# Which place of a step may take the next score product for a maximum, in the first unit of an attention stage

## The chip, the cores and the metric

The kernel runs on one core of one Trainium2 chip. The metric is the device time of one execution, in microseconds (us). It computes two transformer-like layers; the change touches one stage of the first, its attention. The engines in play are TensorE (PE; its weight loads are listed apart as PEld), VectorE (DVE), ScalarE (ACT), GpSimd (POOL) and the queues that issue DMA transfers, among them SyncE's (SP).

## The reference, cut to what matters

The first layer's attention works on x of 2 batches x 2048 tokens x 256, with 16 heads of 16 columns and 32 rotary columns that all heads share:

```
k = (c_kv @ W_k_up).reshape(Bb, Tt, NH, HD);  v = ...;  q = ...
scores = einsum('bqhd,bkhd->bhqk', q, k)
scores = scores + einsum('bqr,bkr->bqk', q_rope, k_rope)[:, None]
scores = scores / sqrt(HD + D_R)
scores = where(causal, -inf, scores)
w = softmax(scores, axis=-1)
attn = einsum('bhqk,bkhd->bqhd', w, v)
return attn @ W_o
```

The softmax is causal: a query sees the keys up to its own. A softmax may subtract any number of a row before the exponential, and this kernel subtracts a row's maximum of approximate scores.

## The kernel before, in words

**Units and steps.** `phase_attention` (from L632) goes over 8 units, each one batch and one group of four heads. The 2048 queries of a unit are four chunks of 512. A unit has 40 steps (`NS`); a step is one chunk `qc` of queries against one block `kb` of 128 keys. The chunks come in the order 2, 3, 1, 0 in all units but the second (unit 1), which has 3, 2, 1, 0 (`ORDER`). So in unit 0 steps 0 to 11 belong to chunk 2, steps 12 to 27 to chunk 3, steps 28 to 35 to chunk 1, and steps 36 to 39 to chunk 0. The last four steps of a chunk lie on the diagonal and have only 512, 384, 256 and 128 columns of queries.

**What TensorE does in a step.** `scores(s, 0)` and `scores(s, 1)` make the transposed scores of two heads each: two matmuls by L1055 and one by L1059 for each of the two heads. The two heads take the upper and the lower 64 rows of the array (in code r = 0 and r = 1), so matmuls of different halves run side by side. Then `weighted` (L1037) multiplies the exponentials of the step before with the values; it needs all 128 rows, so both halves must be through. ScalarE's exponential (L1097) reads the scores, and GpSimd masks the diagonal blocks (L898).

**Maxima ahead.** The number subtracted has to be in the operands before a chunk's first scores. So for each chunk TensorE also makes plain score products (L999), one matmul per pair and half, each into one of three PSUM banks used in turn (`RING` = 3). VectorE reduces each of them to a row maximum (L1175, or L1172 on the diagonal) and so sets its bank free. A unit has 80 pairs (i, block of queries, chunk of keys), so 160 of these products; I call one of them an item, and write 33b for the second half of pair 33. When a chunk's items are reduced comes its turn: VectorE folds them (L1182), TensorE transposes them (L1010), VectorE writes them as f16 (L1186), and the SP queue moves them by DMA into the operands (`shift`, L940 by the trace). The chunk's first scores wait for that DMA (L1055 behind `shift_ld`). All matmuls are in one stream in program order, so a waiting one holds all behind it.

**The planner.** Which item stands at which place of the stream is worked out when the kernel is built, by `schedule()` (from L691). It walks through all steps with a clock `now`, a time `rows[r]` at which each half of the array is through, and a time `reduced` at which VectorE is through with the items so far. `bank_free(slot)` is the time at which the bank of the item three before was reduced, plus 60; `begin_of(x)` is that for an item, and `reduced + 350` for a turn. A step has the places 0 to 7: place 0 ahead of it, places 1 to 6 behind its six pairs of score matmuls (3 and 6 are behind the last of `scores(s, 0)` and `scores(s, 1)`), place 7 behind `weighted`. At each place it issues items as long as they fit: an item behind a score matmul fits if its bank is free by the time its own half is through. At place 6, ahead of `weighted`, an item of the second half fits if its bank is free within 300 of that, and one of the first half if its bank is free within 100 and the bank after it already. If a chunk's turn isn't there when its first step comes, the planner issues all that is missing at place 0, adds 6500 (`FETCH`) for the DMA, and fills the wait with more items. Items of the next unit are allowed from step 6 on (`HEAD_STEP`), up to the end of its second chunk (`AHEAD`). `TODO` holds the result; TensorE (`ahead`, L1012) and VectorE (`ahead`, L1189) both follow it.

In this plan unit 0 opens with items 0a to 30b ahead of step 0, has from then on four items in nearly every whole step (one at place 5, three at place 7), and for step 12 (chunk 3's first) issues five items and the turn at place 0. It ends with 36b of unit 1. Unit 1 ends with 37a of unit 2, unit 2 with 41b of unit 3, and unit 3 with 42a of unit 4. In unit 2 the turn of chunk 3 stands at place 7 of step 10; in units 3 and on at step 7.

Of the kernel before, what the change touches and what calls it, by code (L numbers as in the profile page):

```python
# [631 lines left out]
def phase_attention(nc, g):  # L632
# [17 lines left out]
    def upto(v, m):  # L650
        return sum(2 * TPC * (qc + 1) for qc in ORDER[v][:m])
# [13 lines left out]
    def width(v, k):  # L665
        _, qb, j = PAIRS[v][k]
        return min(CH, (qb + 1) * P - j * CH)
# [10 lines left out]
    def chunk_maxima(v, m):  # L678
        return [("max", v, k, r) for k in range(upto(v, m), upto(v, m + 1)) for r in range(2)]
# [3 lines left out]
    def ticks(w):  # L683
        return w * 0.4167

    def reduce_time(v, k):
        if v == 0 and k in LIFTED:
            return 420
        return width(v, k) / 0.96 + (76 if diagonal(v, k) else 70)

    def schedule():  # L691

        stream = []
        for v in range(NU):
            for m in range(NCH):
                stream += chunk_maxima(v, m) + [("turn", v, m, 0)]
        todo, at = {}, 0
        now = reduced = 0.0
        rows, freed, turned_at = [0.0, 0.0], [], {}

        def may(u, s):
            if at == len(stream):
                return False
            kind, v, n, _ = stream[at]
            return v <= u or (v == u + 1 and s >= HEAD_STEP and n < (AHEAD if kind == "turn" else upto(v, AHEAD)))

        def bank_free(slot):
            return freed[slot - RING] + 60 if slot >= RING else 0.0

        def begin_of(x):  # L710
            return reduced + 350 if x[0] == "turn" else bank_free(len(freed))

        def issue(place):
            nonlocal at, now, reduced
            x = stream[at]
            kind, v, n, r = x
            todo.setdefault(place, []).append(x)
            at += 1
            if kind == "turn":
                now = max(now, *rows, begin_of(x)) + 64  # L720
                rows[:] = now, now
                reduced = max(reduced, now + 400) + 300
                turned_at[v, n] = reduced
                freed.extend([reduced] * (2 if n == NCH - 1 else 1))
            else:
                now = max(now, rows[r], begin_of(x))
                rows[r] = now + ticks(width(v, n)) + 5
                reduced = max(reduced, rows[r] + 217) + reduce_time(v, n)
                freed.append(reduced)

        for u in range(NU):
            for s in range(NS):
                qc, kb = STEPS[u][s]
                t = kb - TPC * qc
                w = CH - max(t, 0) * P
                if kb == 0:
                    m = ORDER[u].index(qc)
                    while (u, m) not in turned_at:
                        issue((u, s, 0))
                    ready = turned_at[u, m] + FETCH  # L740
                    while may(u, s) and max(now, *rows, begin_of(stream[at])) + 300 < ready:
                        issue((u, s, 0))
                    rows[:] = max(rows[0], ready), max(rows[1], ready)
                for i in range(1, 8):
                    if i == 7:
                        now = max(now, *rows) + 200 + ticks(4 * w)
                        rows[:] = now, now
                    else:
                        for r in sorted((0, 1), key=lambda r: rows[r]):
                            now = max(now, rows[r])  # L750
                            rows[r] = now + ticks(w)
                    while may(u, s):
                        x = stream[at]
                        if x[0] == "turn":
                            fits = begin_of(x) <= max(rows)
                        elif i != 6:
                            fits = begin_of(x) <= max(now, rows[x[3]])
                        elif x[3] == 1:
                            fits = begin_of(x) <= max(now, rows[1]) + SLACK + 200
                        else:  # L760
                            fits = begin_of(x) <= max(now, rows[0]) + SLACK and bank_free(len(freed) + 1) <= max(now, rows[0])
                        if not fits:
                            break
                        issue((u, s, i))
        return todo

    TODO = schedule()

    with ExitStack() as c:
# [2033 lines left out]
```

How the kernel before makes its waits and increments, by code:

```python
    def link(self, ins):  # L65
        ins.then_inc(self.sem, 1)
        self.n += 1
        self.eng.wait_ge(self.sem, self.base + self.n)
# [8 lines left out]
def ln_rows(dve, chain, x, tile0, hn, ln, b, it):  # L77
    for t in range(TPC):
        ins = dve.bn_stats(ln.st[:, t, :], x[:, tile0 + t, :])
    chain.link(ins)
    dve.memset(ln.gap[:, :], 0.0)
    for t in range(TPC):
        ins = dve.bn_aggr(ln.mv[:, t, :], ln.st[:, t, :])
    ins.then_inc(ln.var_ready[b], 1)
    dve.wait_ge(ln.root_ready[b], it + 1)
    chain.link(dve.reciprocal(ln.rs[:, :], ln.sd[:, :]))
    for t in range(TPC):
        ins = dve.tensor_scalar(hn[:, t, :], x[:, tile0 + t, :], ln.mv[:, t, 0:1], ln.rs[:, t:t + 1],
                                ALU.subtract, ALU.mult)
    return ins
# [2 lines left out]
def ln_root(act, ln, eps, b, it):  # L95
    act.wait_ge(ln.var_ready[b], it + 1)
    act.activation(ln.sd[:, :], ln.mv[:, :, 1], ACT.Sqrt, bias=eps[:, 0:1]).then_inc(ln.root_ready[b], 1)
# [60 lines left out]
def all_stored(eng, g, kinds, chunks):  # L159
    for kind in kinds:
        for x in range(2):
            eng.wait_ge(g.stored[kind][x], 16 * STORES[kind] * chunks)
# [66 lines left out]
        def own_stored(eng, kind, n):  # L230
            if n >= 2:
                eng.wait_ge(stored[kind][n % 2], 16 * STORES[kind] * (n // 2))
# [23 lines left out]
        @block.gpsimd  # L256
# [13 lines left out]
                pool.wait_ge(w_high, i + 1)  # L270
                pool.tensor_tensor(dst[:, 1, :], src[:, :], dst[:, 0, :], ALU.subtract).then_inc(w_split, 1)
            pool.wait_ge(init_done, 2)
```

## Time and profile before

| | us |
|---|---|
| median of 3 runs | 1664.81 (1660.24 to 1666.56) |
| the profiled execution | 1658.27 |
| its span | 1656.6 |
| TensorE busy in the span | 1486.8 (90%) |
| VectorE busy in the span | 1164.1 (70%) |
| mean granted clock of TensorE | 0.941 |

The attention stage's steps lie from 171.4 us to 1014.8 us of the span. The profile comes from one execution with the hardware profiler. "Idle before" is the time in which an engine had nothing running ahead of an instruction, with the instruction that ended it. Matmuls of the two halves overlap, so their durations are longer than the distance between them, and TensorE can count as busy where one half is idle.

### The profile page before, as it was taken

To read this page: it belongs to the slowest core of one execution; us is meant where nothing else is said; L and a number is where in the kernel's file an instruction comes from. 1 tells how busy PE (TensorE), PEld (TensorE's weight loads), DVE (VectorE), ACT (ScalarE), POOL (GpSimd) and SP (SyncE) were. 2 spreads that over 40 slices of the span, in tenths; PEclk is the share of its full clock that TensorE was granted. 3 is DMA by queue.
4 is the path that set the end of the run, shared out by engine and by line. 5 is a ranking of instruction groups with operands and counts; after the bars stand their busy time and mean duration, and the time that the engine had idled before them with its cause. 6 is when DMAs were issued, how large, how long until landed. Compare 5 with 4: busy or idle time off the path is not lost. (4 is left out here: it accounts for less than half of the span.)

```text
span 1656.6 us, 33664 instructions
## 1 busy us (share of the span) xinstructions
PE 1486.8 (90%) x12297; PEld 785.4 (47%) x12297; DVE 1164.1 (70%) x3308; ACT 925.1 (56%) x1320; POOL 489.8 (30%) x769
## 2 busy tenths in 40 slices
PE   6995889999999999999999998943699979989997
PEld 4441333333333343333333324622588855668775
DVE  3767778888898888888888833961366668414585
ACT  2444556666566666666766774521477745323474
POOL 3482655442212121121211212266200000175333
PEclk9995889999999999999999999975799989999999
DMA  9399432725215134051340143526677600588011
GB/s 324 124 249 238 134 124 91 175 83 98 103 41 105 62 75 124 34 105 61 79 120 34 41 145 113 208 85 119 116 85 91 88 14 3 205 315 295 30 39 52
DMA packets 100452, 191.69 MB, mean 116 GB/s; under 512 B 21976, under 2 KB 66036, under 8 KB 95044
## 3 DMA queue, kind: packets, MB, share of 16 engines
q1 hardware_dynamic: 80324, 113.04, 28.4%
q0 software_dynamic: 17296, 72.87, 13.2%
q10 hardware_dynamic: 2672, 3.62, 0.6%
q8 instruction: 103, 1.69, 0.5%
q14 instruction: 57, 0.47, 0.1%
HBM read 108.58 MB, written 80.81 MB: 114 GB/s over the span
## 5 line engine op out<-in xcount | busy, mean ns | idle before, releaser
L1097 ACT ACTIVATE at_pr<-ps 128x1024 f32<-128x1024 f32 (+3 forms) x640 | 540.8, 893 | 283.5 <-PE ps L1059 281.7
L1175 DVE TENSOR_REDUCE at_mx<-ps 128x1 f32<-128x512 f32 x736 | 462.4, 683 | 65.3 <-PE ps L999 63.7
L1059 PE MATMUL ps<-bq,exw 64*128 64x512 f16 (+3 forms) x1280 | 288.0, 346 | 0.0
L1172 DVE CUSTOM_DVE_ANT_0 at_seen<-ps,later 128x384 bf16<-128x384 f32 (+3 forms) x512 | 229.8, 487 | 28.1 <-PE ps L999 26.4
L898 POOL TENSOR_SCALAR_AFFINE_SELECT at_pr<-at_pr 128x256 f32<-128x256 f32 x256 | 103.7, 412 | 410.4 <-ACT at_pr L1097 407.5
L1055 PE MATMUL ps<-exw 64*128 64x512 f16 (+3 forms) x1280 | 208.6, 350 | 3.3 <-DMA exw<-at_mr 2.8
L1055 PE MATMUL ps<-at_sqk 64*128 64x512 f16 (+3 forms) x1280 | 200.6, 345 | 0.9 <-ACT at_pr L1097 0.8
L999 PE MATMUL ps<-exw 64*128 64x512 f16 (+3 forms) x640 | 169.8, 380 | 23.2 <-DVE at_mx L1172 7.7
L999 PE MATMUL ps<-at_sqk 64*128 64x512 f16 (+3 forms) x640 | 166.6, 350 | 1.8 <-DVE at_mx L1175 1.2
L1037 PE MATMUL ps<-at_pr,at_vl 128*32 128x512 f32 (+3 forms) x1280 | 150.0, 540 | 3.4 <-POOL at_pr L898 3.2
L1037 PE MATMUL ps<-at_pr,exw 128*32 128x512 f32 (+3 forms) x1280 | 150.5, 542 | 0.0
L999 PEld LDWEIGHTS ps<-exw 64*128 64x128 f16 x640 | 45.8, 95 | 160.7 <-DVE at_mx L1175 73.9
L1828 PE MATMUL ps<-ex_hh,exw 128*128 128x256 f16 x624 | 107.0, 277 | 15.7 <-DVE ex_hl L1887 15.7
L1059 PEld LDWEIGHTS ps<-bq,exw 64*128 64x128 f16 x1280 | 97.3, 95 | 40.6 <-issue 0.3
L999 PEld LDWEIGHTS ps<-at_sqk 64*128 64x128 f16 x640 | 45.9, 93 | 141.2 <-DVE at_mx L1175 75.4
L1055 PEld LDWEIGHTS ps<-exw 64*128 64x128 f16 x1280 | 82.8, 95 | 45.6 <-ACT at_pr L1097 7.9
L1055 PEld LDWEIGHTS ps<-at_sqk 64*128 64x128 f16 x1280 | 75.7, 94 | 55.6 <-ACT at_pr L1097 22.8
L2453 PE MATMUL ps<-home,mi_tz 128*128 128x512 f16 (+15 forms) x512 | 93.7, 279 | 6.8 <-DMA mi_tz<-d_z 6.8
L1885 DVE CAST ex_hh<-ex_hf 128x512 f16<-128x512 f32 x78 | 33.4, 429 | 86.8 <-ACT ex_hf L1861 58.7
L1861 ACT ACTIVATE ex_hf<-ps,ex_bias 128x256 f32<-128x256 f32 x156 | 65.4, 471 | 40.1 <-PE ps L1828 23.4
L1828 PE MATMUL ps<-ex_hl,exw 128*128 128x256 f16 x312 | 86.3, 277 | 1.4 <-issue 1.4
L2455 PE MATMUL ps<-home,mi_tz 128*128 128x256 f16 (+15 forms) x512 | 86.1, 222 | 0.0
(325 smaller groups left out, 2294.2 us busy)
## 6 DMA issues: line engine op xcount, KB each, us to landing
d_rows<-at_nil POOLq DMA_DIRECT2D x31, 1064.5 KB, 6.3
mi_tz<-d_z SPq DMA_DIRECT2D x32, 1024.0 KB, 6.8
ex_xr<-d_rows SPq DMA_DIRECT2D x39, 256.0 KB
d_va<-st_va SPq DMA_DIRECT2D x8, 1024.0 KB, 8.7
d_o<-at_oc POOLq DMA_DIRECT2D x32, 256.0 KB, 2.3
at_pw<-in_w POOLq DMA_DIRECT2D x24, 256.0 KB, 3.3
d_w<-at_ph POOLq DMA_DIRECT2D x24, 256.0 KB, 2.4
exw<-d_w SPq DMA_DIRECT2D x8, 768.0 KB
```

The costliest lines, as they stand in the source:

```text
L898: pool.affine_select(block_, block_, pattern=[[0, 2], [1, P]], compare_op=ALU.is_ge, fill=nought, base=0, channel_multiplier=-1).then_inc( ...
L999: pe.matmul(ps[:, bank, 0:hi_ - lo], g.sqk[b][half[r], 0, i, 0, qb * P:(qb + 1) * P], g.sqk[b][half[r], 1, i, 0, lo:hi_], start=True, stop ...
L1037: ins = pe.matmul(ps[32 * h:32 * h + 32, O, off:CH], g.vl[b][:, kb, 32 * h:32 * h + 32], pr[:, n % 2, h // 2, h % 2, off:CH], start=(kb == 0),
L1055: pe.matmul(ps[:, 2 * f + r, off:CH], g.sqk[b][half[r], 1, f, part, k], g.sqk[b][half[r], 0, f, part, q], start=part == 0, stop=False)
L1059: ins = pe.matmul(ps[:, 2 * f + r, off:CH], g.bk[half[r], b, k], g.bq[half[r], b, q], start=False, stop=True)
L1097: act.activation(pr[:, n % 2, f, :, off:CH], ps[:, 2 * f:2 * f + 2, off:CH], ACT.Exp, scale=INV_SCALE).then_inc(exp_done[f], 1)
L1172: ins = dve.tensor_tensor_reduce(seen[:, turn, r, 0:n], src, g.later[:, CH - n:CH], 1.0, LOWEST, ALU.add, ALU.max, dst)
L1175: ins = dve.tensor_reduce(dst, src, AX.X, ALU.max)
L1828: ins = pe.matmul(out(l, cc)[:, o, :], lhs, rhs, start=(i == 0), stop=(i == len(parts) - 1))
L1861: ins = act.activation(hf[l][:, o, :], out(l, cc)[:, o, :], ACT.Relu, bias=bias[:, l, o, cc:cc + 1])
L2453: pe.matmul(out[:, :, d * HD:C], tz[:, x, 0, w], vhl[:, :, tiles, h * HD:(h + 1) * HD], start=(d == 0), stop=False)
L2455: ins = pe.matmul(out[:, 0, d * HD:C], tz[:, x, 1, w], vhl[:, 0, tiles, h * HD:(h + 1) * HD], start=False, stop=(d == NT - 1))
```

## The change

One condition is added at the end of the planner's test. In unit 0 an item or a turn also fits, at any place from 1 to 7, if its bank is free by the time at which the later of the two halves is through, whichever half it needs itself and whatever the bank after it does. All other conditions, the kernel's instructions, their number and their shapes stay.

```diff
@@ -759,6 +759,8 @@
                             fits = begin_of(x) <= max(now, rows[1]) + SLACK + 200
                         else:
                             fits = begin_of(x) <= max(now, rows[0]) + SLACK and bank_free(len(freed) + 1) <= max(now, rows[0])
+                        if u == 0:
+                            fits = fits or begin_of(x) <= max(now, *rows)
                         if not fits:
                             break
                         issue((u, s, i))
```

## Rows read from the trace of the kernel before

**Rows 1.** The costliest groups of the page; last column: idle before, and what ended it

```profile
L1097 ACT ACTIVATE at_pr<-ps 128x1024 f32<-128x1024 f32 (+3 forms) x640 | 540.8, 893 | 283.5 <-PE ps L1059 281.7
L1175 DVE TENSOR_REDUCE at_mx<-ps 128x1 f32<-128x512 f32 x736 | 462.4, 683 | 65.3 <-PE ps L999 63.7
```

**Rows 2.** Windows: stretch, its length, busy time of five engines, PEclk, DMA share, GB/s

```profile
171.40:204.40 33.00, 32.67 (x278) 13.11 (x278) 25.15 (x61) 21.98 (x25) 25.52 (x34) 0.93 0.41 137
204.40:216.35 11.95, 6.50 (x23) 2.07 (x23) 10.57 (x35) 0.00 (x0) 0.16 (x1) 0.61 0.01 1
398.60:509.80 111.20, 108.38 (x979) 40.96 (x977) 95.31 (x280) 69.83 (x85) 24.99 (x50) 0.97 0.32 82
509.80:613.45 103.65, 102.92 (x966) 38.56 (x965) 89.90 (x267) 69.36 (x85) 18.09 (x42) 1.00 0.31 79
```

**Rows 3.** Timeline of DVE in steps 2 to 4 of unit 0

```profile
181.57 2.48 DVE L1175 TENSOR_REDUCE at_mx<-ps 128x1 f32<-128x512 f32 x4 [0.73 <-PE ps L999]
184.40 1.29 DVE L1175 TENSOR_REDUCE at_mx<-ps 128x1 f32<-128x512 f32 x2 [0.35 <-PE ps L999]
```

**Rows 4.** Waits in 175.4 to 204.4 us: who waited for whom, total, times, longest

```profile
DVE at_mx L1175 <- PE ps L999: 6.1, 10, 1.0
```

**Rows 5.** Timeline of PE: a step of unit 0, then a lone item and the `weighted` behind it

```profile
181.15 0.60 PE L999 MATMUL ps<-exw 64*128 64x512 f16 x3
...
182.02 0.81 PE L1055 MATMUL ps<-exw 64*128 64x512 f16 x4
182.46 0.38 PE L999 MATMUL ps<-exw 64*128 64x512 f16 x1
...
182.98 1.06 PE L1037 MATMUL ps<-at_pr,exw 128*32 128x512 f32 x8
183.97 0.50 PE L999 MATMUL ps<-exw 64*128 64x512 f16 x3
...
201.59 0.39 PE L999 MATMUL ps<-exw 64*128 64x512 f16 x1
201.91 0.85 PE L1037 MATMUL ps<-at_pr,exw 128*32 128x384 f32 x8
```

**Rows 6.** Timeline of PE: the turn of chunk 3, then the first scores of steps 12 and 13, unit 0

```profile
208.49 0.47 PE L1010 MATMUL ps<-ident,at_mm 128*128 128x128 f32 x1 [1.70 <-DVE at_mm L1182]
...
216.35 0.72 PE L1055 MATMUL ps<-exw 64*128 64x512 f16 x2
...
220.75 0.75 PE L1055 MATMUL ps<-exw 64*128 64x512 f16 x4
```

**Rows 7.** Timeline of PE: from the end of unit 0 into unit 1

```profile
288.27 0.64 PE L1037 MATMUL ps<-at_pr,exw 128*32 128x256 f32 x8
...
290.37 0.61 PE L999 MATMUL ps<-at_sqk 64*128 64x512 f16 x2 [0.37 <-DVE at_mx L1175]
290.69 0.51 PE L1055 MATMUL ps<-at_sqk 64*128 64x512 f16 x2
```

**Rows 8.** Waits of DVE in 216.35 to 295.6 us

```profile
DVE at_mx L1175 <- PE ps L999: 6.5, 14, 1.2
DVE at_seen L1172 <- PE ps L999: 3.1, 4, 1.0
```

**Rows 9.** Timeline of PE: the turn of chunk 3 and step 12, unit 2

```profile
423.40 0.33 PE L1010 MATMUL ps<-ident,at_mm 128*128 128x128 f32 x1
...
430.47 0.72 PE L1055 MATMUL ps<-exw 64*128 64x512 f16 x2
```

**Rows 10.** Timeline of PE: the same turn and the last step before step 12, unit 3

```profile
525.89 0.33 PE L1010 MATMUL ps<-ident,at_mm 128*128 128x128 f32 x1
...
536.22 0.64 PE L1037 MATMUL ps<-at_pr,at_vl 128*32 128x256 f32 x8
```

**Rows 11.** Windows: the first steps after unit 2's gap, and items ahead of unit 0

```profile
430.50:434.60 4.10, 4.10 (x27) 1.64 (x26) 3.38 (x13) 1.56 (x2) 0.00 (x0) 0.50 0.00 2
136.10:160.60 24.50, 13.45 (x48) 2.92 (x48) 22.15 (x88) 15.50 (x16) 8.81 (x4) 0.50 0.92 185
```

## The prediction

> **What bounds the kernel now.** I first read the busy shares: TensorE is busy for 90% of the span. Of the costliest groups, the exponentials' idle time is time in which ScalarE waited for TensorE, and the reductions of the maxima (L1175) wait for TensorE too [rows 1]. So ScalarE is out, and the question is TensorE against VectorE. Then I cut the attention into stretches [rows 2]. Unit 3 (509.8 to 613.45 us, first `weighted` to first `weighted`) takes 103.65 us with TensorE busy for 102.92: TensorE bounds it. VectorE has 13.75 us to spare there. In unit 2 the same steps take 111.2 us, 7.55 more. Unit 0 is worst: steps 0 to 11 end at 204.4, and until 216.35 us TensorE makes only items and one turn. In that gap VectorE is busy for 10.57 of 11.95 us, most of it needed before the turn or waiting for the DMA behind it. So unit 0 is bound there by VectorE's backlog, and yet in the 33 us before, VectorE was busy for 25.15 only. Why? The timeline of VectorE shows one gap after the other, of 0.73 and 0.35 us and so on, each ended by an item's matmul [rows 3]; together they make 6.1 us in 175.4 to 204.4 [rows 4]. Each lies where `weighted` runs: in a step nothing is issued between the item at place 5 and the three behind `weighted`, which holds TensorE for about 1 us [rows 5]. The banks run dry meanwhile.
>
> **What the change removes, adds and moves.** No instruction is added or removed. 1280 products, 1280 reductions and 32 turns stay, and only the stream's order changes. The new clause is weaker than the old one at places 1 to 5 only by the difference of the two halves, but at place 6 it lifts the demand that the bank after be free as well. So items move ahead of `weighted`. I followed the planner's arithmetic through steps 0 to 3, to learn which items go where (for prices I use the trace). In step 0 item 31b goes from place 4 to 3, and 32a, 32b and 33a fit at place 6; step 1 has 34b at 2, 35a at 4, 35b at 6; step 2 has 37b at 4, 38a at 6; step 3 has 39b at 2, 40a at 4, 40b at 5, 41a at 6, and two behind `weighted`. The old plan ends step 3 with 39a, the new one with 42a: six items more in four steps. VectorE idles for 0.5 us in these steps, and from step 2 on for nothing. From here on I extrapolate.
>
> *Chunk 3's turn in unit 0.* It stands at 208.49 us and the first scores behind it at 216.35, 7.86 us later, through the DMA [rows 6]; nothing in that distance changes. I can take out only what VectorE idled ahead of the turn. The gaps between reductions in the timeline, from the 0.72 us before 177.32 to the last at 198.33, are nine with a sum of 5.1 us (the row of 6.1 us takes in one at the start that stays) [rows 3, 4]. Less the 0.5 us left and some 0.3 us by which a turn now waits for a place of a running step, 4.3 us. TensorE reaches step 12 later than before, by 9 steps with five items for four and a little loss (below), some 2.5 us; at 207 us it still waits for the DMA until about 212, so that costs nothing. Bounds: 3.3 us (a turn may wait for a whole `weighted`, 1.06 us [rows 5]) to 5.1. Gain 4.3.
>
> *What is late next.* At 212 us VectorE has done as much as it had at 216.35 before, so unit 0 goes on from the same state, earlier. In the rest of the unit VectorE waits 6.5 and 3.1 us for items [rows 8]. Not all of it can go: some lies at turns. I take 6.5 us, or 11 items at about 0.6 us each (2.48 us for four [rows 3]). TensorE's steps get longer by the two terms below, about 5 us in which VectorE does eight more, less three for the shorter wait at the unit's end: some 15 items of lead. Bounds 5 and 20.
>
> *Unit 1's start.* The last step of unit 0 ends at about 288.9 us, and the first scores of unit 1 are at 290.69 [rows 7]; like the others they wait for the DMA behind a turn. With a lead of several items this wait vanishes. It had some eight items in it, so the gain is not 1.8 us in full; I take 1.6, bounds 1 and 2.3.
>
> *Unit 2.* Its turn stands at 423.40 and step 12 begins at 430.47, again 7.07 us behind [rows 9], while in unit 3 the turn stands at 525.89 and the `weighted` ahead of step 12 at 536.22, 10 us later, with nothing to wait for [rows 10]. Unit 2 begins at item 37b, unit 3 at 42a: nine items. Four items go with a step of about 2.8 us, so nine come 6.4 us earlier, and 15 are enough. The lead should last through unit 1, since a step there takes four items whatever the lead is. Then unit 2 is like unit 3 and gains 7.5 us (111.2 less 103.65 [rows 2]); half of that is the gap itself and the rest the slow clock behind it [rows 11]. Bounds: 0 and 8.3.
>
> *What it costs.* The 15 items are TensorE's work moved into unit 0. Four score matmuls, two in each half, take from 182.02 to 182.46, so two of one half follow each other at 0.22 us [rows 5], so an item costs 0.11 if the other half is filled too: 1.6 us, of which the last unit gives some 0.5 back. And an odd number of items ahead of `weighted` leaves a half idle: a lone item at 201.59 has `weighted` behind it at 201.91 [rows 5]. That is up to 0.22 us a step, or nothing if the number is even. For the 28 steps from 12 on I take 0.13 us each, 3.6 us, bounds 0 and 6.2.
>
> *Cover.* GpSimd's masks and weight splits, the DMA of `load` and the exponentials keep their order on their own engines. A later `weighted` gives ScalarE more time. GpSimd sat idle over the whole wait at step 12 (0.16 us busy in 11.95 [rows 2]), so 4.3 us less there hurts nothing.
>
> Sum: -4.3 - 1.6 - 7.5 + 1.6 - 0.5 + 3.6 = -8.7 us. On the profiled execution's 1658.27 us that is 1649.6. The median shown is 6.5 us over that execution, and I expect the same spread after: 1664.8 - 8.7 = 1656.1 us.
>
> **The clock and a rule that speaks against it.** The granted clock was 0.61 over the gap of unit 0 and 0.50 in the first steps behind unit 2's gap, against 1.00 in unit 3 [rows 2, 11]; that is 1.2 against 2.4 GHz. It was also 0.50 in 136.1 to 160.6 us, where TensorE made items alone and was busy for 13.45 of 24.5 us [rows 11]. In the changed unit 0 TensorE works at VectorE's pace and may wait for a bank in every step. The Trainium skill, page "TensorE: Matmul & The Clock Gate", section "A second HAM failure mode: psum-queue depth-cycling", says that a kernel which cycles through PSUM banks can idle in small pieces often enough for the clock to swing between its two levels. This trace agrees in the stretch of items alone; no row of it shows whether it holds for steps with scores between. By that rule the change would cost as in the third rival below.
>
> **Rivals.** *The lead is lost.* Only the first turn and unit 1's start gain, because unit 1's own plan falls back to the state of before, which it does if the lead shifts an item behind a turn. Against it: the plans of units 3 and 4 begin at about the same item. For it: unit 1 has another order. -4.3 - 1.6 + 1.6 + 3.6 = -0.7 us: 1664.
>
> *Waits in front of `weighted` (the other side).* An item placed at place 6 waits for its bank on the chip, and since the matmuls stand in one stream, `weighted`, the next step's scores and through them the exponentials wait too. The planner supposes that a bank is free 60 ns behind its reduction; if VectorE runs behind the plan, each step pays. Near unit 1's start such a wait was 0.37 us [rows 7]. Over 28 steps that is 10.4 us. If unit 2's gap goes as forecast, the sum is +1.7; with the lead lost, as such waits leave VectorE no more done per us, it is +9.7 us: 1674. It decides against the change from 0.31 us a step with the gap gone, from 0.03 with the lead lost. Against it: four reductions take 2.48 us on the chip and 2.41 in the plan.
>
> *The clock falls in unit 0.* Step 12 of unit 0 ran behind the gap on the slow clock and took from 216.35 to 220.75, 4.4 us [rows 6], for the usual 2.8: 1.6 us more. For half of the 28 steps that is 22 us: +14 with the forecast's sum, 1679.
>
> *More than forecast.* The halves come out even and nothing is lost ahead of `weighted`: without 3.1 of the 3.6 us, and 0.8 more at the turn, -12.6: 1652.
>
> *It doesn't do what it says.* If the planner's clock ran far off the chip's, places would mean little; its step takes 2.66 to 2.78 us and the chip's 2.82 (181.15 to 183.97 [rows 5]), so I give this no chance of its own.
>
> **Chances.** Forecast (-5 to -11 us) 0.42; more than forecast 0.15; lead lost, in part or whole 0.28; waits ahead of `weighted` 0.12; clock 0.03. A measurement of this kernel can tell about 0.5% from no change, 8.3 us, and my forecast lies right at that bound. Faster by more: half of the forecast's 0.42 and nearly all of the 0.15 and a little of the third, 0.38. Slower by more: a third of the waits' cases with the clock's, and some for what I haven't seen in a plan extrapolated from four steps, 0.12. Same: 0.50. Range 1645 to 1671 us; within the forecast's case alone, 1653 to 1660.
>
> **What would show it.** In the trace after: item matmuls between the last scores and `weighted` in whole steps of unit 0; VectorE's waits for L999 in 175.4 to 204.4 us down from 6.1 us to about 1; the turn at about 204 and step 12 at about 212 us; no wait ahead of unit 1; unit 2 at 103 to 104 us with a turn at least 8 us ahead of step 12 and a clock of 1.00; whole steps of unit 0 about 0.2 to 0.3 us longer. The prediction is wrong if unit 2's gap is still there (then about 1664), or if `weighted` follows bank waits of over 0.3 us.

## The result, and the profile after

The changed kernel took 1647.69 us (median of 5, 1642.82 to 1650.89) against 1662.11 (median of 5) for the kernel before: ratio 0.992, 95% interval 0.9898 to 0.9943, or 9 to 17 us less. Its profiled execution took 1647.42 us with a span of 1645.6, 11.0 less than before. The forecast was 1656.1. The sign was right and the time lies inside the range of 1645 to 1671 us, but it lies below 1653, where the forecast's own case ends: the gain is 14.4 us by the medians and 11.0 by the spans, where I had forecast 8.7. That is the case "more than forecast", to which I gave 0.15, and no change had the highest chance of all, 0.50.

The attention holds the whole difference. From the first `weighted` of unit 0 to the end of the last one of unit 7 it took 837.3 us before and takes 825.4 now; both kernels start it within 0.3 us of each other, and the rest of the kernel differs by 1.1 us the other way. By units (first `weighted` to first `weighted`, us):

| unit | 0 | 1 | 2 | 3 | 4 to 6, each | 7 |
|---|---|---|---|---|---|---|
| before | 118.2 | 103.0 | 111.2 | 103.7 | 102.9 | 92.5 |
| after | 115.0 | 102.9 | 102.9 | 103.4 | 102.9 | 92.6 |

Windows of the changed kernel, the first, second and the last two answering to [rows 2] (columns as there); the third is the first step after the gap, and answers to the slow window of [rows 11]:

```profile
171.40:204.40 33.00, 32.64 (x253) 10.90 (x249) 28.53 (x67) 20.78 (x23) 22.57 (x29) 0.90 0.39 135
204.40:211.42 7.02, 4.83 (x40) 1.92 (x38) 6.57 (x24) 0.75 (x3) 1.25 (x4) 0.82 0.01 2
211.42:215.26 3.84, 3.84 (x17) 1.30 (x17) 3.24 (x12) 1.02 (x1) 0.00 (x0) 0.50 0.01 2
394.96:497.87 102.91, 102.60 (x966) 38.66 (x964) 89.35 (x266) 69.56 (x85) 24.72 (x50) 1.00 0.34 89
497.87:601.27 103.40, 102.67 (x966) 38.68 (x964) 89.40 (x266) 69.57 (x85) 18.31 (x43) 1.00 0.31 80
```

VectorE was busy for 25.15 of 33 us ahead of the gap and is for 28.53 now. Unit 2 now looks like unit 3, its clock back from 0.97 to 1.00. Why VectorE is busier shows in TensorE's timeline: most of one step of unit 0 and the start of the next. An item stands right ahead of `weighted` (189.67, then 189.99), where in [rows 5] the last item is ahead of the last score pair, and the step has five items for four:

```profile
187.90 0.39 PE L1001 MATMUL ps<-exw 64*128 64x512 f16 x2
188.12 0.38 PE L1057 MATMUL ps<-exw 64*128 64x512 f16 x2
188.34 0.38 PE L1001 MATMUL ps<-exw 64*128 64x512 f16 x1
...
189.67 0.39 PE L1001 MATMUL ps<-exw 64*128 64x512 f16 x1
189.99 1.07 PE L1039 MATMUL ps<-at_pr,exw 128*32 128x512 f32 x8
190.98 0.39 PE L1001 MATMUL ps<-exw 64*128 64x512 f16 x2
```

(The change adds two lines, so L999, L1010, L1037, L1055, L1059, L1175 and L1182 are L1001, L1012, L1039, L1057, L1061, L1177 and L1184 now.) VectorE's waits for items in 175.4 to 203.56 us, against 6.1 in [rows 4]:

```profile
DVE at_mx L1177 <- PE ps L1001: 1.5, 2, 1.3
DVE at_seen L1174 <- PE ps L1001: 0.7, 2, 0.5
```

So the reductions that the second turn needs are all done, and folded, at 203.13 us instead of 208.22. The turn itself stands behind a `weighted` and comes 1.2 us later. These lines of two timelines, VectorE's and TensorE's, answer to [rows 6]:

```profile
203.13 0.22 DVE L1184 TENSOR_REDUCE at_mm<-at_mx 128x16 f32<-128x64 f32 x1
```

```profile
204.35 0.33 PE L1012 MATMUL ps<-ident,at_mm 128*128 128x128 f32 x1
...
211.42 0.72 PE L1057 MATMUL ps<-exw 64*128 64x512 f16 x2
```

And the start of unit 1, answering to [rows 7]: its first scores (names `at_sqk`) come 0.01 us behind the first item after `weighted`, with no wait between.

```profile
287.23 0.64 PE L1039 MATMUL ps<-at_pr,exw 128*32 128x256 f32 x8
287.80 0.28 PE L1001 MATMUL ps<-at_sqk 64*128 64x256 f16 x1
287.81 0.71 PE L1057 MATMUL ps<-at_sqk 64*128 64x512 f16 x4
```

Unit 2's turn, answering to [rows 9], now has a full 10.3 us and five steps between it and the `weighted` ahead of step 12, as unit 3 had in [rows 10]:

```profile
410.80 0.33 PE L1012 MATMUL ps<-ident,at_mm 128*128 128x128 f32 x1
...
421.13 0.64 PE L1039 MATMUL ps<-at_pr,exw 128*32 128x256 f32 x8
```

### The profile page after: what moved, and what is told of

The parts are those of the page before. It is cut to its first block and busy times, and to the rows that moved or that the text cites. A ratio compares the mean times of both kernels' runs of the same rounds, so it can differ in the third digit from the quotient of the medians.

```text
span 1645.6 us, 33664 instructions
## 1 busy us (share of the span) xinstructions
PE 1483.0 (90%) x12297; PEld 783.0 (48%) x12297; DVE 1163.8 (71%) x3308; ACT 924.5 (56%) x1320; POOL 487.7 (30%) x769
## 5 line engine op out<-in xcount | busy, mean ns | idle before, releaser
L1177 DVE TENSOR_REDUCE at_mx<-ps 128x1 f32<-128x512 f32 x736 | 462.9, 684 | 56.9 <-PE ps L1001 55.2
L1061 PE MATMUL ps<-bq,exw 64*128 64x512 f16 (+3 forms) x1280 | 290.3, 346 | 0.0
L900 POOL TENSOR_SCALAR_AFFINE_SELECT at_pr<-at_pr 128x256 f32<-128x256 f32 x256 | 103.2, 410 | 418.8 <-ACT at_pr L1099 416.2
L1057 PE MATMUL ps<-exw 64*128 64x512 f16 (+3 forms) x1280 | 209.6, 349 | 1.4 <-DMA exw<-at_mr 1.4
L1057 PE MATMUL ps<-at_sqk 64*128 64x512 f16 (+3 forms) x1280 | 199.7, 345 | 0.7 <-ACT at_pr L1099 0.6
L1001 PE MATMUL ps<-exw 64*128 64x512 f16 (+3 forms) x640 | 172.3, 376 | 19.9 <-PEq L582 7.8
L1001 PE MATMUL ps<-at_sqk 64*128 64x512 f16 (+3 forms) x640 | 165.4, 350 | 0.6
L1039 PE MATMUL ps<-at_pr,at_vl 128*32 128x512 f32 (+3 forms) x1280 | 150.0, 540 | 3.4 <-POOL at_pr L900 3.2
L1039 PE MATMUL ps<-at_pr,exw 128*32 128x512 f32 (+3 forms) x1280 | 150.6, 543 | 0.0
L1001 PEld LDWEIGHTS ps<-exw 64*128 64x128 f16 x640 | 46.3, 95 | 161.5 <-DVE at_mx L1177 76.3
L1061 PEld LDWEIGHTS ps<-bq,exw 64*128 64x128 f16 x1280 | 98.0, 94 | 39.4 <-issue 0.8
L1001 PEld LDWEIGHTS ps<-at_sqk 64*128 64x128 f16 x640 | 45.6, 93 | 140.1 <-DVE at_mx L1177 75.7
L1057 PEld LDWEIGHTS ps<-at_sqk 64*128 64x128 f16 x1280 | 75.8, 94 | 54.9 <-ACT at_pr L1099 21.6
L1057 PEld LDWEIGHTS ps<-exw 64*128 64x128 f16 x1280 | 80.5, 95 | 41.7 <-ACT at_pr L1099 6.7
```

The costliest lines, as they stand in the source:

```text
L900: pool.affine_select(block_, block_, pattern=[[0, 2], [1, P]], compare_op=ALU.is_ge, fill=nought, base=0, channel_multiplier=-1).then_inc( ...
L1001: pe.matmul(ps[:, bank, 0:hi_ - lo], g.sqk[b][half[r], 0, i, 0, qb * P:(qb + 1) * P], g.sqk[b][half[r], 1, i, 0, lo:hi_], start=True, stop ...
L1039: ins = pe.matmul(ps[32 * h:32 * h + 32, O, off:CH], g.vl[b][:, kb, 32 * h:32 * h + 32], pr[:, n % 2, h // 2, h % 2, off:CH], start=(kb == 0),
L1057: pe.matmul(ps[:, 2 * f + r, off:CH], g.sqk[b][half[r], 1, f, part, k], g.sqk[b][half[r], 0, f, part, q], start=part == 0, stop=False)
L1061: ins = pe.matmul(ps[:, 2 * f + r, off:CH], g.bk[half[r], b, k], g.bq[half[r], b, q], start=False, stop=True)
L1177: ins = dve.tensor_reduce(dst, src, AX.X, ALU.max)
```

## The experiments

Runs of the same kernel differ by some 0.4% and the chips by 2% (the kernel before took 1630, 1629 and 1659 us on those used here), so a ratio of totals tells 3 us at best. Within one trace the attention is far steadier. The changed kernel's took 825.4 us and, on another chip, 825.0, and units 4 to 6 took 102.9 us in every trace where their plan is unchanged. Unit 0 is less steady, 114.1 to 115.0 us in the traces that share the changed kernel's plan for it. "Attention" below is that stretch, from the first `weighted` to the end of the last, in one profiled execution. A kernel's plan is read from `TODO`.

**Theory.** VectorE's idle time over `weighted` was the cause of three waits of TensorE: at step 12 of unit 0, at the start of unit 1, and at step 12 of unit 2, where only the lead in items counts that units 0 and 1 hand over. TensorE pays in unit 0. **Rivals:** the first turn alone carries the gain; places 1 to 5 carry it; items ahead of `weighted` cost nothing, or cost more than they bring.

### Which steps

```diff
-                        if u == 0:
+                        if u == 0 and s < 12:
```

> The added condition holds only in steps 0 to 11 of unit 0. The plan then has unit 0's second turn at place 7 of step 10 as in the changed kernel, but unit 0 ends at item 1.36b and unit 2 begins after 2.37a, as before the change. Theory (the gain is made of three waits, and unit 2's goes by the lead): step 12 of unit 0 begins 4.5 to 5 us earlier, the gap in unit 2 stays at 5.5 us with the slow clock behind it, attention ends 4.5 to 5 us earlier than before: ratio 0.9972. Rival (the first turn brings everything behind it into step, unit 2's gap too): 10 us or more earlier, ratio 0.994 or less.

Ratio 0.9948 (0.9928 to 0.9967). Attention 832.5 us, 4.8 less than before. Unit 0 takes 113.6 us (118.2 before), unit 2 111.1 (111.2), with the gap as it was:

```profile
423.13 0.33 PE L1012 MATMUL ps<-ident,at_mm 128*128 128x128 f32 x1
...
424.04 0.64 PE L1039 MATMUL ps<-at_pr,exw 128*32 128x256 f32 x8
430.20 0.72 PE L1057 MATMUL ps<-exw 64*128 64x512 f16 x2
```

The total came out 3 to 4 us better than the attention explains, which is at the edge of what totals tell; its interval leaves out the ratio I expected (0.9972) and takes in the rival's (0.994). The trace excludes the rival: the attention gained 4.8 us and not 10, and unit 2's gap is there.

```diff
-                        if u == 0:
+                        if u == 0 and s >= 12:
```

> The added condition holds only from step 12 of unit 0 on. The plan keeps the second turn at step 12 (place 0), as before the change, but unit 0 ends at item 1.43a as in the changed kernel. Theory: no gain at step 12; the rest of unit 0 costs 3 to 4 us for 13 items more and idle halves and gets 2.4 us back at the start of unit 1; unit 2 takes 102.9 us for 111.2. Attention ends 7.2 us earlier: ratio 0.9957. Rival (first turn carries the gain): attention ends within 1.5 us of before or later, ratio 1.000 to 1.002.

Ratio 0.9946 (0.9927 to 0.9965). Attention 831.0, 6.3 less than before (7.2 expected: the gap at step 12 was 0.3 us longer, and the last unit 0.8). Unit 0 takes 119.7, unit 2 102.9. So either half of the steps gives its own part, and the two parts, 4.8 and 6.3, make 11.1 of the 11.8 us. The larger one has nothing to do with the first turn.

### Which places

```diff
-                        if u == 0:
+                        if u == 0 and i == 6:
```

> The added condition holds only at place 6, ahead of weighted. Theory (VectorE's idle time lay over weighted, and only items ahead of it can end it): nearly the whole change, attention ends 11 to 12.5 us earlier, ratio 0.9925. Rival (places 1 to 5, where the later half now counts, bring a good part): half of it or less, ratio 0.996 or more.

Ratio 0.9912 (0.9888 to 0.9935). Attention 826.9: 10.4 less, just short of the 11 to 12.5 expected. Unit 0 is even better than with the whole change, 112.3 us, but unit 1 took 106.7; more on that below.

```diff
-                        if u == 0:
+                        if u == 0 and i != 6:
```

> The added condition holds at all places but 6. Theory: the second turn of unit 0 stays at step 12 and the unit ends at 1.36b as before; within 1 us of the kernel before, ratio 0.9995. Rival: as above, half of the change's gain or more, ratio 0.996 or less.

Ratio 1.0005 (0.9985 to 1.0026). Attention 840.6: 3.3 us more than before, a miss. The plan has items one place earlier in unit 0 and no lead comes of it, but whole steps take 2.92 us for 2.83, which fits items that wait 0.09 us for a bank there, but I have it from start times alone. Unit 1 took 104.9 for 103.0, with a 2.0 us wait for a mask where it was 1.04. So place 6 makes the gain, and places 1 to 5 bring none by themselves. Beside place 6 they cost unit 0 some 2 us; the attention as a whole still came out 1.5 us shorter with them, as unit 1 took 102.9 us for 106.7.

### The lead taken away again

```diff
+            if u == 1 and v == 2 and kind == "max" and n > 34:   # in may()
+                return False
```

> The changed kernel once more, on the chip of the other three kernels here. From the first weighted of unit 0 to the last of unit 7 it took 825.5 us before; both theories expect 825.5 within 1.5 us, and the ratio to the kernel before 0.992 again.

> The changed kernel, but unit 1 may not issue items of unit 2 beyond 2.34b, so the lead is given up at the end of unit 1 and unit 2's second turn stands at place 7 of step 10 as before the change. Unit 0 is that of the changed kernel. Theory (unit 2's gap goes by the lead at unit 2's start): the gap of 5.5 us is back with the slow clock behind it, unit 2 takes 111 us for 102.9, unit 1 is 1.5 us shorter for 16 items fewer, unit 3 is as before; attention 831 to 832.5 us, ratio to the kernel before 0.9962. Rival (the gap goes because units 0 and 1 end earlier, or by what the changed order does to the DMA queues): unit 2 stays at 103 to 105 us, attention 824 to 826.

The changed kernel again: ratio 0.9911 (0.988 to 0.9942), attention 825.0. One of its six executions took 3649 us; I have no cause for it, and the median doesn't hang on it. With the limit: ratio 0.9974 (0.9951 to 0.9997), attention 832.0, in the range. Unit 2 takes 110.8 us for 102.9; its window, then the turn and the first scores of step 12, 7.28 us apart:

```profile
396.49:507.28 110.79, 107.98 (x978) 40.71 (x976) 95.71 (x284) 69.76 (x85) 24.74 (x49) 0.97 0.32 82
```

```profile
421.29 0.33 PE L1014 MATMUL ps<-ident,at_mm 128*128 128x128 f32 x1
...
428.57 0.72 PE L1059 MATMUL ps<-exw 64*128 64x512 f16 x2
```

Units 0 and 1 ended as early as in the changed kernel, so the rival is out. That fewer items (15 by the plan; I had written 16) would make unit 1 1.5 us shorter failed: it took 102.8.

The same limit at 28 for 34:

> As the last, but the limit is 2.28b; unit 2's second turn then stands at place 0 of step 12, with items yet to be made there. Theory: the gap grows by about 0.6 us for each item missing beyond the last case: unit 2 at 115 to 117 us, unit 1 at 99.5 to 101; attention 834 to 836.5 us, ratio 0.999 to 1.000. Rival: as above, no gap.

Ratio 1.0002 (0.9983 to 1.0021), attention 838.7, unit 1 101.5, unit 2 118.0. It is over my range by 2 us. For 12 items fewer than with the limit at 34 unit 2 grows by 7.2 us, 0.6 each, as a reduction takes. With all of unit 0's gain in place, taking the lead away once, later, costs as much as the whole change brings. Both limits leave unit 2 with less than the kernel before had: it enters behind 34b and 28b, where it was 37a.

```diff
+            if u == 0 and v == 1 and kind == "max" and n > 39:   # in may()
+                return False
```

> The changed kernel, but unit 0 may not issue items of unit 1 beyond 1.39b: a lead of 6 items over the kernel before instead of 13; unit 1 makes it up again and ends at 2.41b. Theory: unit 2 has no gap (102.9 to 103.2 us), as only the lead at its start counts; units 0 and 1 together as in the changed kernel within 1.5 us; attention 825 to 827, ratio 0.991. Rival (each item of lead of unit 0 counts): the gap is back by half, attention 828.5 or more.

Ratio 0.9942 (0.9919 to 0.9966), attention 828.4, outside my range by 1.4 us. But unit 2 takes 103.2 us and has no gap. That doesn't say that half of the lead is enough for it: by the plan unit 1 makes 164 items for 158 and enters unit 2 behind 41b, one item short of the changed kernel. It says that unit 1 can make up what unit 0 leaves out. What is lost is lost in unit 0 (115.5: its last two steps are 1.1 us longer) and in unit 1 (104.8 for 102.9, with six items more and a wait for a mask of 1.60 us for 1.05). The rival's figure came out by another way than the rival's.

### What TensorE pays

```diff
-                        if u == 0:
+                        if True:
```

> The added condition holds in all units, not only the first. Theory (TensorE pays for items ahead of weighted with an idle half and for waits for a bank, 0.07 us a step as in the changed unit 0, and from unit 2 on there is no VectorE wait to win back): units 2 to 6 take 105.5 us each for 102.9, attention 15 us longer than the changed kernel, ratio to the kernel before 1.000 to 1.003. Rival (such items cost nothing, since the halves come out even over a few steps): units 2 to 6 at 102.9, ratio 0.992.

Ratio 1.008 (1.0049 to 1.0112): slower than the kernel before. Attention 850.0, 25 us over the changed kernel where I expected 15. Units 4 to 6 take 107.0 us each for 102.9, with the same 160 items. Their windows, this kernel's unit 4 and then the changed kernel's, and the waits of VectorE for items in the former:

```profile
618.75:725.78 107.03, 106.39 (x966) 37.86 (x965) 89.17 (x268) 69.47 (x85) 18.44 (x43) 1.00 0.30 77
```

```profile
601.27:704.19 102.92, 102.61 (x966) 38.65 (x965) 89.37 (x266) 69.57 (x85) 18.42 (x43) 1.00 0.31 79
```

```profile
DVE at_mx L1177 <- PE ps L1001: 12.6, 13, 6.0
```

VectorE's work is the same and it idles all the more, in one stretch of 6.0 us, since its lead reaches the planner's limit of two chunks. TensorE counts as busy for 3.8 us more with the same matmuls: busy is what the records say, but halves are idle or waiting in them. That is 4.1 us a unit, 0.10 us a step; how it divides between idle and waiting halves I did not measure. So the condition is worth nothing where no wait is to be won back, and it is `u == 0` that makes the change a gain.

```diff
-                            fits = fits or begin_of(x) <= max(now, *rows)
+                            fits = fits or begin_of(x) <= max(now, *rows) + 200
```

> In unit 0 an item also fits if its bank is free up to 200 ns after the later half is through, so the plan has TensorE wait for banks ahead of weighted and elsewhere; it puts 22 more items into unit 0, no item at step 12, and a lead up to 1.55b. The rival of the prediction made strong. Theory: VectorE sets when the second turn of unit 0 comes (it idles for under 1.5 us ahead of it in the changed kernel), so step 12 begins at most 1 us earlier; each step waits up to 0.2 us more for a bank, and the lead buys nothing from unit 2 on. Attention 836 to 845 us for 825.0 of the changed kernel; ratio to the kernel before 1.000 to 1.008. Rival (waits ahead of weighted are hidden): 825 or less, ratio 0.991.

Ratio 1.0046 (1.003 to 1.0062), attention 842.0, in the range, but by two errors that cancel. The plan puts 25 more items into unit 0 (I had written 22). The gap at step 12 is gone, yet unit 0 takes 136.9 us, with many steps of 4 to 5 us: a wait of up to 0.2 us a step was expected, and nine whole steps of chunk 3 take 4.4 us on average for 3.0. And the lead did buy something: units 2 to 6 make 156 items for 160 and take 101.3 to 102.4 us for 102.9, and from unit 1 on the attention is 5.4 us shorter. One of those long steps, of PE (score matmuls L1057 and L1061, items L1001):

```profile
235.43 0.60 PE L1057 MATMUL ps<-exw 64*128 64x512 f16 x2
236.02 0.39 PE L1001 MATMUL ps<-at_sqk 64*128 64x512 f16 x1
236.02 0.60 PE L1061 MATMUL ps<-bq,exw 64*128 64x512 f16 x2
236.62 0.39 PE L1001 MATMUL ps<-at_sqk 64*128 64x512 f16 x1
236.94 1.06 PE L1039 MATMUL ps<-at_pr,exw 128*32 128x512 f32 x8
```

Items start 0.60 us apart, which is VectorE's pace for a reduction (0.60 us from start to start there), and the score matmuls start with them though they need no bank of VectorE's. This is the prediction's rival of waits in front of `weighted`, seen when the planner asks for it. The page hides it: no idle time stands at these lines, and PE reads as busy for 134.26 of 136.94 us. I read it from start times alone.

### A wait that nobody had asked about

Every kernel up to here waits in unit 1 for a mask at the chunk's first diagonal, 0.35 to 2.46 us, the kernel before as well (1.04). A window and TensorE's timeline at its start, first of the kernel with place 6 only, then of the changed kernel (in brackets: the idle time ahead of the instruction in us, and what ended it; the clock is the third figure from the right):

```profile
327.50:332.50 5.00, 4.98 (x45) 2.03 (x45) 3.17 (x9) 1.27 (x3) 1.39 (x4) 0.66 0.07 26
```

```profile
327.52 1.07 PE L1039 MATMUL ps<-at_pr,at_vl 128*32 128x512 f32 x8 [2.09 <-POOL at_pr L900]
```

```profile
327.00:331.00 4.00, 3.97 (x54) 1.64 (x56) 1.71 (x11) 1.84 (x5) 1.62 (x5) 1.00 0.10 37
```

```profile
327.03 1.06 PE L1039 MATMUL ps<-at_pr,at_vl 128*32 128x512 f32 x8 [1.05 <-POOL at_pr L900]
```

GpSimd makes four weight splits ahead of that mask, and one of them waits 10.1 us in the changed kernel for its fetch:

```profile
304.36 0.72 POOL L853 DMA_DIRECT2D at_pw<-in_w  x1
315.15 1.03 POOL L864 TENSOR_TENSOR at_ph<-at_pw,at_one 128x512 f16<-128x512 f32 x1 [10.06 <-DMA at_pw<-in_w]
```

```diff
-    SPLITS = {(0, 2): 6, (0, 3): 7, (0, 1): 2, (1, 3): 4, (1, 2): 3, (2, 3): 2}
+    SPLITS = {(0, 2): 6, (0, 3): 7, (0, 1): 2, (1, 3): 2, (1, 2): 3, (2, 3): 4}
```

> The changed kernel with GpSimd's weight splits moved: two of the four that stand ahead of unit 1's first diagonal go to unit 2. In all traces so far weighted waits there for a mask, 1.0 to 2.1 us. Theory (GpSimd comes late, as its fetch waited 10 us for the load of unit 2's heads): the wait is gone and unit 1 takes 101.3 to 102 us for 102.9; attention 823.5 to 824.3. Rival (the wait is for ScalarE's exponential behind which the mask stands): unit 1 stays at 102.9.

Ratio 0.9911 (0.9889 to 0.9934). Attention 823.9, unit 1 101.75, both in range, and no wait for a mask is left there.

```profile
291.81:393.56 101.75, 101.70 (x965) 38.87 (x963) 87.87 (x266) 69.36 (x85) 35.69 (x62) 1.00 0.39 106
```

> The added condition at place 6 only, and the splits moved as in the last: the version that should beat both kernels. With place 6 alone unit 0 took 112.3 us for 114.3, and unit 1 lost it again to the masks (106.7). Theory: unit 0 112.3, unit 1 103 to 104.5, attention 822 to 824; ratio 0.990. Rival (unit 1's loss there has nothing to do with the splits): unit 1 at 106 or more, attention 826 or more.

Ratio 0.9924 (0.9897 to 0.9951), attention 823.5, unit 0 112.2 and unit 1 103.3: as expected, and 1.5 to 2.0 us under the changed kernel's attention, but only 0.4 under that of the last kernel, which has the whole change. In unit 1 it saves 3.4 us where the wait was 2.1; the rest, 1.3 us, fits the clock (5.0 us at 0.66 lose up to 1.7 us, an estimate), but no run separates the two. The totals can't tell these two kernels from the changed one.

## Why the prediction was right, and where it was off

**The cause was right.** Idle time of VectorE over `weighted`, ended by items at place 6: with place 6 alone 10.4 of 11.8 us come, without it none, and taking the lead away in unit 1 brings unit 2's gap back. The three places where it would show were right too, and so was the step "the lead should last through unit 1": the plan enters unit 2 behind item 42a where it was 37a.

**The turn, right by two errors.** Forecast -4.3 us for the turn, measured -4.14. I kept 0.5 us of VectorE's idle time and gave 0.3 to a turn that waits for a place. The reductions ended 5.09 us earlier, all that was to be had, and the turn waited 1.2 us behind a `weighted`, more than the bound I took from its 1.06 us. "Nothing in that distance changes" was wrong: from the turn to the first scores it took 7.07 us for 7.86 before. 0.15 us of that is the transpose, on the full clock (0.33 us) where it ran on the slow one (0.47). Step 12 began 4.93 us earlier.

**What the gaps waited for: not the DMA.** The kernel's description and the prediction have the first scores behind a gap wait for the DMA behind the turn. At step 0 of unit 0 they do: the last update of that DMA's semaphore comes at 171.36 us and the scores at 171.40. At step 12 it comes at 212.85 us and the scores 3.50 us later (2.76 in the changed kernel, 208.66 and 211.42); at unit 1's start it was 3.48 us and at step 12 of unit 2 2.92. In between TensorE makes items and waits for VectorE. Two lines of the timeline of the kernel before, for step 0 and for the item 0.10 us ahead of step 12's scores, and what TensorE's items waited for in 208 to 217 us, where no wait for a DMA is listed:

```profile
171.40 0.61 PE L1055 MATMUL ps<-exw 64*128 64x512 f16 x2 [2.78 <-DMA exw<-at_mr]
...
216.25 0.39 PE L999 MATMUL ps<-exw 64*128 64x256 f16 x1 [0.30 <-DVE at_mx L1175]
```

```profile
PE ps L999 <- DVE at_mx L1175: 2.9, 7, 0.6
```

It is the planner that puts the items there. It adds 6500 ns for the DMA (`FETCH`) and fills that time at place 0, with 16 items behind the turn in unit 0 before, where from the first issue to the last update it took 3.5 to 3.6 us at these gaps. So some 3 us of each gap were the plan's. Whether a smaller `FETCH` alone would have brought part of this gain is a rival that no run tested; the items would then have to be made later. It also accounts for the shorter distance: from VectorE's write of the turn's result to the first scores VectorE does the same 24 instructions in 6.57 us, before (first) and after, and only its idle time is less.

```profile
209.00:216.35 7.35, 4.45 (x17) 1.41 (x16) 6.57 (x24) 0.00 (x0) 0.00 (x0) 0.50 0.01 2
```

```profile
204.71:211.42 6.71, 4.52 (x36) 1.73 (x35) 6.57 (x24) 0.66 (x2) 1.02 (x3) 0.81 0.01 2
```

**Unit 1's start.** Forecast -1.6, measured -2.4 (4.67 us from `weighted` to `weighted` before, 2.30 now): the wait, and items that no longer had to stand in it.

**Unit 2.** Forecast -7.5, measured -8.3. I had taken unit 3's 103.65 as what is left, but the steady value is 102.9, which I had given as the bound.

**What it costs, the largest miss.** The lead was forecast at 15 items and is 13 (1.36b to 1.43a). I priced them and the idle halves at 1.6 and 3.6 us. From the `weighted` that ends the gap to the end of the unit, unit 0 took 75.8 us before and 76.85 now; with the 2.4 us won at the unit's end the gross cost is 3.4 us, of which 13 items at 0.11 are 1.4. So the halves cost 2.0 us, 0.07 a step where I had taken 0.13. The 0.11 is an estimate, but steps bear it out: between two `weighted` of whole steps I find 2.40 us with no item (kernel with 200 ns of slack), 2.61 with two, 2.83 with three and with four, and 3.09 with five. An item that leaves its half alone costs as much as two. The halves' 2.0 us were within my bounds of 0 and 6.2 but not at their middle, for the clause lets items fit only where the bank is free before the later half is through. The kernel with the condition everywhere shows the price to be no constant: 0.10 us a step in a unit that has no wait to win back. And the 0.5 us that the last unit was to return never came (92.5 and 92.6 us): its lead is 42 pairs in both.

Summed, the forecast's terms of 8.7 us were 11.8 in the attention. From the first `weighted` of unit 0 to the one that ends the gap it is 4.3 us less, as forecast (4.8 in the changed kernel's second trace): step 12 began 4.93 us earlier, but the unit began 0.28 earlier too, and step 12 took 0.32 longer to its `weighted`. Unit 1's start gave 0.8 more, unit 2 0.8 and the cost 1.8; the last unit took 0.5 away, and units 1 and 3 were 0.1 and 0.3 us shorter. So the gain came out larger above all because I had priced the cost too high. Of what I had given for "more than forecast", even halves and a better turn, the halves came about halfway (2.0 us for the 3.6 of the forecast and the 0.5 of that case), the turn not at all.

**The rivals.** The lead was not lost. Waits in front of `weighted` did not decide: TensorE's recorded waits for VectorE in unit 0's steps stay under 0.3 us in all, and the steps' lengths leave little room for hidden ones, though with 200 ns more slack they do decide. The clock stood at 1.00 from 178.1 to 208.8 us and from 215.7 us on in the changed kernel; it was 0.50 over the gap's end and step 12 and up to 178.1 us, in the unit's first steps. The kernel before was at 0.50 until 176.3 us too. In a kernel that issued items in VectorE's pace (slack of 200 ns) it stayed at 1.00 over the whole of unit 0. The Trainium skill ("TensorE: Matmul & The Clock Gate", "A second HAM failure mode: psum-queue depth-cycling") reports of another kernel that cycling through PSUM banks made the clock swing between its two levels. This case's traces show no such swing where scores stand between the items. In the stretch of items alone, where I wrote that the trace agrees, the clock was low (0.50) but did not swing either. "GpSimd hurts nothing" was too quick. It was right for the wait at step 12 of unit 0, but in unit 1 GpSimd was behind already, and TensorE waited 1.05 us before and after.

## What to carry to other kernels

If one engine's total load is below another's and the other still waits for it, look for where its idle time lies in each step, and put its feed just ahead of the long instruction over which it idles. A planner should accept that the bounding engine loses something only as long as a wait is to be won back: the same condition gave 12 us in one unit's steps and cost 4 us in each unit that had no such wait. Price a lead not where it is made but at the next point that waits for it. And read from the trace what ends a wait before you name it: here the plan's constant for a DMA, not the DMA, made the later part of each gap.

## What the runs showed of the hardware that I had not expected

A single wait of 2.09 us was followed by a lower granted clock of TensorE. In the kernel with place 6 only it stood idle so long ahead of a `weighted`, and the mean of the 5 us behind was 0.66 against 1.00 over the 4 us behind the changed kernel's wait of 1.05 us; unit 1 took 3.4 us more than without the wait. The kernel without place 6 shows the same, 2.00 us and 0.66. But length alone does not decide: in the kernel with 200 ns of slack a wait of 2.46 us at the same place was followed by 1.00. What made the difference no run shows. A row's idle time is thus not always the full price of a wait.

A matmul behind a waiting one has no idle time of its own in the trace, and the recorded 0.38 us of a matmul, where two of one half can follow each other at 0.22 us, cover much of what lies between. In the kernel with 200 ns of slack PE read as 98% busy in a unit that took 22 us too long; only start times 0.60 us apart, equal in both halves, gave it away.
